# Two chained cross-attentions: maximum scores on 32 rows of the array, values and denominators from the same matmuls, eight PSUM banks in one ring

## The reference, cut to what matters

```python
# layer 0, per batch: x, y are 128 x 512
energy = (w_qk y)^T (w_qk x)                         # 512 x 512
attention = softmax(energy, -1); attention /= 1e-7 + attention.sum(1)
x_v = w_v x + b_v;  x_r = x_v attention              # 128 x 512
x = x + relu(w_t (x - x_r) + b_t)
# layer 1, per batch: hidden = x (128 rows), encoder = y (128 rows)
q = x Wq + bq; k = y Wk + bk; v = y Wv + bv          # 32, 8 and 8 heads of 16
scores = q k^T / 4 + mask;  attn = softmax(scores, -1)
out = (attn v) Wo + bo + x
out = (out - mean) * rsqrt(var + 1e-6) * gamma + beta
```

## Time and profile before

| | |
|---|---|
| median of 3 runs | 890.93 us (890.02 to 891.68) |
| profiled execution | 890.17 us |
| its span (first to last instruction) | 888.4 us |
| mean granted clock of TensorE | 0.974 of full |
| busy: TensorE, VectorE, GpSimd, ScalarE | 828.3, 668.7, 534.4, 454.6 us |

### The profile page before, as it was taken

The page is one execution under the profiler, slowest core; times in us unless marked ns, Lnnn a source line. Parts: engine busy times, 40 slices in busy tenths (PEclk is TensorE's granted clock), DMA queues, the critical chain, the costliest instruction groups (busy, mean ns, idle before and its releaser), DMA issues.

```text
span 888.4 us, 18179 instructions
## 1 busy us (share of the span) xinstructions
PE 828.3 (93%) x5291; PEld 646.3 (73%) x5291; DVE 668.7 (75%) x1144; ACT 454.6 (51%) x998; POOL 534.4 (60%) x724
## 2 busy tenths in 40 slices
PE   4559999999999999999999999999999999999773
PEld 3558696777869687787869777786869777786631
DVE  5337787887878787887878788787878788786744
ACT  1715546373745637274654737374564737364240
POOL 4573738385774929486683938477592938564403
PEclk9779999999999999999999999999999999999977
DMA  8223232343414224343323234342413334231310
GB/s 288 71 66 78 56 77 74 89 106 90 100 41 110 57 82 106 89 100 87 84 53 100 71 89 106 89 100 66 100 50 89 91 89 104 67 78 39 95 46 24
DMA packets 49914, 75.44 MB, mean 85 GB/s; under 512 B 9824, under 2 KB 27872, under 8 KB 49760
## 3 DMA queue, kind: packets, MB, share of 16 engines
q1 hardware_dynamic: 49888, 75.12, 32.7%
HBM read 24.75 MB, written 8.39 MB: 37 GB/s over the span
## 4 chain that ended last, share of the span: by engine, by line
PE 88%; SPq 3%; POOL 2%; DMA 2%; ACT 2%; issue 2%; DVE 1%; POOLq 0%; ACTq 0%
PE wide L632 13%; PE wide L715 8%; PE den L727 7%; PE wide L691 7%; PE outt L727 6%; PE gen L747 4%; PE gen L669 3%; PE gen L671 3%; PE gen L670 3%; PE gen L749 3%; PE gen L748 3%; PE wide L617 3%; PE wide L619 3%; PE wide L618 3%; SPq L336 3%; PE wide L605 2%
## 5 line engine op out<-in xcount | busy, mean ns | idle before, releaser
L1212 DVE TENSOR_REDUCE maxima<-wide 128x4 f32<-128x512 f32 x256 | 165.7, 685 | 20.3 <-PE wide L691 19.1
L966 ACT ACTIVATE prob<-wide 128x512 f32<-128x512 f32 x256 | 138.1, 601 | 65.8 <-PE wide L715 61.5
L499 POOL TENSOR_TENSOR mv<-bns 128x4 f32<-128x4 f32 x16 | 3.2, 202 | 204.2 <-DVE bns L1264 204.2
L632 PEld LDWEIGHTS wide<-ta,att 128*128 128x128 f32 x1024 | 119.9, 193 | 3.2 <-issue 0.4
L632 PE MATMUL wide<-ta,att 128*128 128x130 f32 x1024 | 121.5, 277 | 0.1
L1243 DVE RECIPROCAL at<-den 128x512 f32<-128x512 f32 x32 | 107.2, 3350 | 5.0 <-PE den L727 3.6
L905 ACT ACTIVATE att<-wide,negmax 128x512 f32<-128x512 f32 x128 | 87.4, 685 | 42.4 <-DVE negmax L1157 42.3
L715 PE MATMUL wide<-qstack,kstack 112*128 112x512 f32 x256 | 97.3, 439 | 7.2 <-DMA qstack<-mrep 6.9
L691 PE MATMUL wide<-kbh,qh 128*128 128x512 f32 x256 | 99.9, 422 | 0.4 <-DVE ql L1205 0.2
L1157 DVE TENSOR_REDUCE negmax<-wide 128x1 f32<-128x512 f32 x128 | 86.0, 683 | 11.8 <-PE wide L619 9.7
L465 POOL TENSOR_TENSOR ta<-ta,cb_s 128x516 f32<-128x516 f32 x64 | 78.2, 1233 | 0.1
(11 more groups left out here) (141 smaller groups left out, 2080.6 us busy)
## 6 DMA issues: line engine op xcount, KB each, us to landing
qstack<-qh SPq DMA_DIRECT2D x128, 128.0 KB, 2.4
xs<-in_x SPq DMA_DIRECT2D x16, 512.0 KB, 3.9
ys<-in_ctx SPq DMA_DIRECT2D x16, 512.0 KB, 3.5
kstack<-kbh SPq DMA_DIRECT2D x128, 64.0 KB, 2.0
qstack<-ql SPq DMA_DIRECT2D x64, 128.0 KB, 2.4
out_x<-late SPq DMA_DIRECT2D x32, 256.0 KB, 2.2
kstack<-kpl SPq DMA_DIRECT2D x64, 64.0 KB, 2.0
qstack<-mrep SPq DMA_DIRECT2D x128, 32.0 KB, 2.0
```

Of the source, the lines that this page charges most:

```text
L632: last = mm(o, att[:, j, n, bass.ts(m, P)], ta[:, j, n, 0:BW], start=n == 0, stop=n == KC - 1)
L966: nc.scalar.activation(prob[:, kv], wide[:, slot(plan, f"st{j}{kv}")], exp_f).then_inc(sem["prob_done"], 1)
L1212: nc.vector.tensor_reduce(maxima[:, j, 0, 2 * half:2 * half + 2, 2 * g:2 * g + 2], wide[:, slot(plan, f"mx{j}{g}{half}")].rearrange("x (p ...
```

## The change

- Maximum scores: `max_scores` handles a group g for both batches. For each of the four key-head pairs p it multiplies only the 32 rows of this pair, `qh[32p:32p+32]`, with `kph` (two heads, each masked to its 16 rows), 256 columns for each batch, into one bank per p. 16 matmuls of 128 rows x 512 columns become 32 of 32 rows x 256 columns; the number of banks that VectorE reduces stays 16. `kbh` (two operations of 1024 elements) becomes `kph` (one of 512).
- One split, one spread and one masking of maxima for both batches (4 DMAs of 32 rows that write both batches' places, instead of 8 of 16 rows); `scores` is 128 rows deep; the row selectors at the bottom of `kstack` differ for the two batches.
- `denominators` is gone. `v2` holds the 16 channels and 16 ones interleaved, so `values` gives, in one bank for even and one for odd heads, values and denominators; even and odd heads are not accumulated. ScalarE copies both banks to `sides` (`keep_sums`), SP gathers the denominators with two DMAs (`dens`) and the odd values with a third, VectorE takes the reciprocal of `dens` and the product from SBUF.
- The order of heads in the output weights is changed to suit (on load).
- PSUM is one ring of 8 banks (`banks`), with other orders on all engines. `out_project` of j = 1 moves to the next iteration (stage 3).
- The high parts of x and y move from GpSimd to ScalarE, `x2_low` from VectorE to GpSimd; the low attended part (`at_low`) is on VectorE as before.
- Ramp: x is loaded first; the constants and small weights are issued by ScalarE's queue; iterations -1 and 0 and the last two have orders of their own (`first_iteration`, `last_iteration`); the splits of the first x and y are shared between engines; the exponential's table is loaded with a first small activation; the flag is gathered by a DMA and reduced on VectorE instead of two matmuls.

The diff, cut to its core (`banks` for `wide`/`gen`, the setup and the lists of uses are left out):

```diff
             def max_scores(q, plan, i, g, masked):
+                wait(pe, "ql_done", q, g)
+                for j in range(2):
+                    for p in range(KV // 2):
+                        name = f"mx{g}{p}"
+                        if j == 0:
+                            wait_slot(pe, plan, name, i, have=("ql_done", -1, g))
+                        rows = slice(32 * p, 32 * p + 32)
+                        last = mm(banks[:, slot(plan, name), 2 * P * j:2 * P * (j + 1)], qh[rows, j, g], kph[rows, j],
+                                  start=True, stop=not masked)
-                last = mm(o, qh[:, j, g], kbh[:, j, 4 * half:4 * half + 4], start=True, stop=not masked)
...
+            def gather_denominators(q, j):
+                wait(sp, "side_done", q, 2 * j + 1)
+                for odd in range(2):
+                    sp.dma_start(dens[odd:P:2], sides[1 - odd:P:2, odd]).then_inc(dens_in, 16)
+            def gather_values(q, j):
+                sp.wait_ge(dens_in, (2 * q + j + 1) * 32)
+                sp.dma_start(sides[1:P:2, 0], sides[1:P:2, 1]).then_inc(values_in, 16)
...
-            def weigh(q, j, dst, operand, done):
-                wait(pe, "prob_done", q, 8 * j + 7)
-            def denominators(q, j):
-                weigh(q, j, den, lambda kv, odd: ones_eo[:, odd], "den_ps")
+            def values(q, plan, i, j, odd):
+                wait(pe, "prob_done", q, 8 * j + 4 * odd + 3)
+                for p in range(KV // 2):
+                    last = mm(banks[32 * p:32 * p + 32, slot(plan, name)], v2[:, j, 2 * p + odd], prob[:, 2 * p + odd],
+                              start=True, stop=True, tile_position=(0, 32 * p))
...
+            def keep_sums(q, plan, j, odd):      # ScalarE
+                wait(act, "o_ps", q, 2 * j + odd)
+                nc.scalar.activation(sides[:, odd], banks[:, slot(plan, f"o{j}{odd}")], copy_f
+                                     ).then_inc(sem["side_done"], 1)
...
             def inverse_denominators(q, j):
-                wait(dve, "den_ps", q, j)
-                nc.vector.reciprocal(at[:], den[:]).then_inc(sem["dinv_done"], 1)
+                dve.wait_ge(dens_in, (2 * q + j + 1) * 32)
+                nc.vector.reciprocal(dens[:], dens[:]).then_inc(sem["dinv_done"], 1)
             def weigh_out(q, j):
-                tt(at[:], outt[:], at[:], ALU.mult).then_inc(sem["at_done"], 1)
+                dve.wait_ge(values_in, (2 * q + j + 1) * 16)
+                tt(at[:], sides[:, 0], dens[:], ALU.mult).then_inc(sem["at_done"], 1)
```

More of the change, by code:

```diff
@@ L61, with ring @@
 C_ONES = C_KVMASK + KV
-C_GMASK = C_ONES + 2 * 2 * HD
+C_GMASK = C_ONES
 C_ODD = C_GMASK + G
 C_MODD = C_ODD + 2
-C_LN = C_MODD + 2
+C_LN = C_MODD + 4
 LN_CONSTANTS = (1.0 / N, LN_EPS, 0.25, -0.5, 1.5)
 C_ALL = C_LN + len(LN_CONSTANTS)
+FIRST_GEN_USES = (
+)
+FIRST_WIDE_USES = (
[4 rows of a table added]
+)
 GEN_USES = (
-    [("q0", 2), ("q1", 2), ("q2", 2), ("q3", 2), ("et0", 1), ("et1", 1), ("m0", 2), ("r0", 2), ("k", 1),
-     ("r1", 2), ("m1", 2), ("z0", 0), ("z1", 0), ("v", 1), ("wo0", 2), ("vt0", 1), ("vt1", 1), ("wo1", 2)]
 )
 WIDE_USES = (
[8 rows of a table removed]
-)
[L84 to L92, removed]
-    plan = {}
[L94 to L101, removed]
[9 rows of a table added]
+)
+LAST_GEN_USES = (
+)
+LAST_WIDE_USES = (
[6 rows of a table added]
+)
+GEN_SLOTS, WIDE_SLOTS = 0, 8
+def ring(uses, first, slots, stages, past):
+    at, held = past
+    held = {bank: (name, back + 1) for bank, (name, back) in held.items()}
+    plan = {}
+    for name, stage in uses:
+        if stage in stages:
+            bank = first + at
+            plan[name] = (bank, *held.get(bank, (None, 0)))
+            held[bank] = (name, 0)
+            at = (at + 1) % slots
+    return plan, (at, held)
 def build_xattn(nc, x, ctx, mask, w_qk, w_v, w_t, b_t, Wq, Wk, Wv, Wo, bo, gamma, beta, columns, consts, out):
@@ L614, in energy @@
                 wait_slot(pe, plan, name, i)
-                o = wide[:, slot(plan, name)]
+                o = banks[:, slot(plan, name)]
                 a, b = yh[:, j, bass.ts(n, P)], yl[:, j, bass.ts(n, P)]
@@ L629, in attend @@
                     m = 2 * h + half
-                    o = wide[:, slot(plan, name), half * 256:half * 256 + BW]
+                    o = banks[:, slot(plan, name), half * 256:half * 256 + BW]
                     for n in range(KC):
@@ L707, in scores @@
                     pe.wait_ge(kstack_in, (q + 1) * 16 * 3 * (KV // 2))
-                if kv % 2 == 0:
-                    if j == 0:
-                        pe.wait_ge(qstack_in[kv // 2], (q + 1) * 16 * 3)
-                    pe.wait_ge(maxrow_in[j][kv // 2], (q + 1) * 16)
+                odd, p = kv // 4, kv % 4
+                if j == 0 and odd == 0:
+                    pe.wait_ge(qstack_in[p], (q + 1) * 16 * 3)
+                    pe.wait_ge(maxrow_in[p], (q + 1) * 16)
                 wait_slot(pe, plan, name, i)
-                o = wide[:, slot(plan, name)]
-                rows = 96 + MROWS
-                last = mm(o, kstack[0:rows, j, kv], qstack[0:rows, kv // 2, j], start=True, stop=not masked)
+                o = banks[:, slot(plan, name)]
+                last = mm(o, kstack[:, j, 2 * p + odd], qstack[:, p, j], start=True, stop=not masked)
                 if masked:
@@ L1216, in max_split, with score_max @@
-            def max_split(q, j):
-                wait(dve, "max_done", q, 8 * j + 7)
-                wait(dve, "m_ps", q - 1, j)
-                heads, minus_high = maxima[:, j, 0], maxima[:, j, 1]
-                high, low = mrow[:, j, :, 0], mrow[:, j, :, 1]
+            def score_max(q, plan, g, p):
+                wait(dve, "mx_ps", q, 4 * g + p)
+                if g == 0 and p == 0:
+                    wait(dve, "mrow_done", q - 1, 2)
+                nc.vector.tensor_reduce(maxima[:, 0, p, :, 2 * g:2 * g + 2],
+                                        banks[:, slot(plan, f"mx{g}{p}")].rearrange("x (j o s) -> x j o s", j=2, o=2),
+                                        AX.X, ALU.max, negate=True).then_inc(sem["max_done"], 1)
@@ L1221, in max_split @@
+            def max_split(q):
+                wait(dve, "max_done", q, 15)
+                wait(dve, "m_ps", q - 1, 0)
+                heads, minus_high = (maxima[:, t].rearrange("x p j m -> x (p j) m") for t in range(2))
+                high, low = (mrow[:, :, :, t].rearrange("x p j m -> x (p j) m") for t in range(2))
                 red = nc.vector.tensor_reduce
                 red(high, heads.unsqueeze(3), AX.X, ALU.max).then_inc(sem["mrow_done"], 1)
-                wait(dve, "mrow_done", q, 3 * j)
+                wait(dve, "mrow_done", q, 0)
```

1157 lines of the change are left out of this document (726 added, 431 removed), and 27 rows, old and new, of tables (FIRST_WIDE_USES, LAST_WIDE_USES, WIDE_USES).

## The result

The changed kernel takes 921.25 us (median, 920.74 to 923.01) against 890.47 in the same comparison: 1.034 times, 95% interval 1.032 to 1.036. I had forecast 827 with a range of 793 to 862; it is slower, by 3.4%. Its profiled span is 919.3 us, with a mean granted clock of 0.932.

The account below looks back on a forecast made before the run. TensorE's list of matmuls was taken to bound each period (50.56 us), afterwards a loop through VectorE and DMAs (47.7). Ramp 51 + 15 x 47.7 + tail 58.5 = 825, plus 1.8 around it: 827 us, range 793 to 862.

Parts of the forecast that it names:

- The ramp: Start of the kernel until the first matmul of iteration 1: 51 us for 66.69 before, bounds 44 and 62.
- VectorE's half of the loop: VectorE's first energy maximum through score maxima, split, spread and mask: 18.1 us, inside a loop of 47.7.
- the second rival: Packed maximum-score matmuls do not run together: TensorE's list 47.6 us, loop 48.2, total 834 us; chance 0.14.
- The landing of the maxima: Maxima's DMAs ahead of the scores: 2.0 us from issue to landing, with four times the bytes; first scores at 21.
- The clock: TensorE's clock stays full; only the slower rival had slow matmuls after a wait over 4 us, costing 2.7 us.
- the slower rival: Maxima and denominator DMAs each land at 3.4 us and the clock falls: loop 53.4, total 912 us; chance 0.05.
- the tail: Last iteration, without energies, to the end of the kernel: 58.5 us for 60 before.
- The products: VectorE's products of values and reciprocals, both operands in SBUF: 0.69 us each taken, bounds 0.69 and 1.21.
- the lock: VectorE operations with two SBUF inputs wait for a GpSimd operation beside them: loop about 50 us, only in the range.
- The other engines: Busy time a pair: ScalarE 32.5 us, GpSimd 28.3, VectorE 37.9; none becomes the bound by its sum.
- TensorE's list: TensorE's matmuls in a period: 50.56 less 3.5 (denominators), 0.24 (spread) and 2.0 (maximum scores), giving 44.8 us.
- The bounds: Unknown costs around the likeliest case: 795 to 855 us for loops of 45.8 to 49.5.

Follow-up runs that it names:

- run 3: Changed kernel with 14 idle matmuls on TensorE just ahead of the wait for the maxima: 901.45 us.
- run 10: Kernel of run 6 with idle matmuls on TensorE in the last iteration only, ahead of the first query, first score and output projection: 860.37 us.
- run 2: Changed kernel with the maxima at half the bytes, eight transfers instead of four, y's load still ahead of them: 909.51 us.
- run 8: Kernel before the change, with only the load of y moved ahead of the first half's maxima: 938.34 us, 1.056 times.
- run 9: Changed kernel with y's load split into two transfers of 256 KB, one ahead of the maxima, one behind: 898.91 us.
- run 1: Changed kernel with the load of the next y issued behind the maxima's transfers instead of ahead: 868.33 us, 0.976 times the kernel before.
- run 6: Kernel of run 1 with the same work reordered, GpSimd's closing operations and the stores moved into the next iteration: 865.11 us.
- run 5: Kernel of run 1 with GpSimd's two closing operations on one column instead of 512: 861.36 us.

## Why the prediction was wrong

Point by point, from the sum 51 + 15 x 47.7 + 58.5 + 1.8.

- **The ramp** was right: iteration 1 starts at 50.89.
- **VectorE's half of the loop** was right up to the transfers. From the first energy maximum at 0: first score maximum 4.75 (I said 5.1), end of the split 16.5 (16.9), masking done 17.9 (18.1), SP's first maxima 18.6 (18.5). The packed maxima run together, eight in 0.5 to 0.7 us; the second rival is out.
- **The landing of the maxima** is the step that failed: 2.0 us in the sum, 4.3 measured. I had written that y's load lies behind the stack's DMAs and ahead of the maxima, and charged it with its issue, 0.45 us, alone; for the landing I took 2.0, the row of transfers that had y behind them, and noted "four times the bytes" without a price. First scores came at 23.9 instead of 21. Moving y alone brings them to 20.6 (409.86 to 430.49), my number.
- **The clock.** I gave half clock only to the slower rival, as from a wait of over 4 us. A wait of 3.4 to 4.0 does it here, and costs 20 us (run 3); the same in the tail, 4.5 us (run 10), which is most of what 64.2 us had above my 58.5. It needs less: after 2.48 us (run 2) and 2.13 (run 8) the clock fell as well, after 2.07 once of twice (run 9), and in run 10 after 0.69. The length of the wait alone doesn't decide, since 2.34 (run 8) and 0.73 (run 10) left it at 1.00. The slower rival (912 us) had the right mechanism and was nearest in time, but let every transfer of the loop land at 3.4 us; only the maxima were late, the denominators' landed after 2.0.
- **The products.** I chose the lower bound, 0.69, by the row of the same operation. That row read one operand from PSUM; the changed one reads both from SBUF, like the low part, whose own row has 1.21. The right row was the one with the same operands. With the low attended part (1.72 for 1.21) it makes 28.7 us from first score to the next energy maximum in run 1, for my 26.7; in run 6, without the lock, it is 26.6. The Trainium skill (SBUF — State Buffer, "Who interferes with whom") says that a VectorE instruction with two SBUF inputs contends with a GpSimd instruction that reads SBUF; I had put that into the range only. Products that end 0.55 us after GpSimd's operation, and take 0.69 without one, agree with it.
- **The other engines** were near: in a period of the changed kernel ScalarE is busy 30.8 us (I said 32.5), GpSimd 29.4 (28.3), VectorE 40.2 (37.9, without the 2.1 of the lock).
- **TensorE's list** is 46.8 us busy in run 6 and not 44.8. By the distances of starts, values with denominators took 7.1 and take 3.9 (I said -3.5), maximum scores 4.4 and 2.5 (-2.0), the spread 0.56 and 0.33: -5.4 together, for my -5.7. So the parts removed were right, and other groups have grown. The most is in the scores, 4.3 to 5.0, for which I had put nothing: the first ones start one by one behind the landings of the maxima. The rest: projections of x 3.9 to 4.3, of the energies' z 1.4 to 1.7, of the queries 5.9 to 6.2, residual transposes 0.7 to 1.0. I subtracted from a list whose groups followed one another without a gap; now more of them start behind another engine. That these handovers are the cause is argued from the distances, not tried.
- **The bounds.** By my own terms a loop of 45.8 us gives 798 and one of 49.5 gives 854, where I wrote 795 and 855; it changes nothing in the range.

The 53.6 us of a mean period (from 50.89 to 855.08) against my 47.7 are 5.9. Moving y brings it to 50.2 (51.28 to 804.23), undoing the lock to 49.8 (50.70 to 797.47). Of the 94 us between forecast and result 53 are y with its clock. The other 41, by run 1's trace: about 24 are its middle periods (49.3 for 47.7: the lock and TensorE's longer list), 5.5 the tail (64.0 for 58.5), and some 13 lie in the loop outside the middle periods. The first three are 50.3, 52.5 and 50.0 us from first score to first score, and the second and third begin at a clock of 0.79 for 8 us (130.79 and 183.25); no run took these 13 us apart.

## What to carry to other kernels

When a reordering puts a load ahead of a transfer that an engine waits for, price it in bytes and not in its issue: here 512 KB were 2.0 us of landing from one queue and 2.4 from the other. A landing time from the old trace holds only with the same transfers in flight ahead of it, and a duration from the old trace only for the same places of both operands. After a change that shortens the bounding list, ask first which wait it opens on TensorE; that wait costs its length, and then often the clock. Read more than one period, since the clock behind equal waits differed.

## What the runs showed of the hardware that I had not expected

- The landing of 128 KB rose with the bytes ahead: 2.3, 3.1 and 4.3 us for 0, 256 and 512 KB, and 4.7 when the 512 KB came from ScalarE's queue.
- The clock behind a stall in a dense loop: a wait of 3.43 us was followed by 3.9 us at a clock of 0.58, one of 2.48 by 4.2 us at 0.50 (run 2), one of 2.13 by 0.57 and one of 2.34 by 1.00 (run 8), one of 2.07 by 0.59 or by 1.00 (run 9), one of 0.69 by 8 us at 0.79 and one of 0.73 by 1.00 (run 10). Fourteen idle matmuls in the place of the wait kept it at 1.00 (run 3).
- A VectorE product with both operands in SBUF took 0.69 us alone (all 32 of run 5), and 1.60 and 1.34 beside a GpSimd operation of 1.28 us, ending 0.55 us after it both times.
